# A fused gated MLP and per-sequence adapter kernel: reordered first steps and tail, and another order of ScalarE's two halves of each weight chunk

## The reference

```python
# layer 0: gated MLP with a conditioned norm; 127-level activations, ternary down weights
scale = cond @ norm_w.T + 1.0
ms = jnp.mean(x * x, axis=-1, keepdims=True)
h = x * (scale[:, None, :] * jax.lax.rsqrt(ms + EPS))
val, gate = jnp.split(h @ up_w.T, 2, axis=-1)
h = val * jax.nn.gelu(gate, approximate=False)
y = act_quant(h) @ weight_quant(down_w).T
x = y + x
# layer 1: adapter whose weights are generated from cond for each sequence
dWd = ((h_lang @ Wdd.T + bdd) * DELTA_SCALE).reshape(B, BN, D)
dWu = ((h_lang @ Wdu.T + bdu) * DELTA_SCALE).reshape(B, D, BN)
down = jax.nn.relu(jnp.einsum('bld,bnd->bln', x, Wd + dWd) + bd)
out = x + jnp.einsum('bln,bdn->bld', down, Wu + dWu) + bu
```

## Time and profile before

| | us |
|---|---|
| median of 3 runs | 473.05 (473.02 to 473.46) |
| profiled execution, its own time | 473.57 |
| its span, first to last instruction | 471.8 |
| busy in the span: PE | 464.3 (98%) |
| busy: DVE | 386.4 (82%) |
| busy: ACT | 364.3 (77%) |
| busy: POOL | 269.1 (57%) |

### The profile page before, as it was taken

The page is one execution under the profiler, slowest core; times in us unless marked ns, Lnnn a source line. Parts: engine busy times, 40 slices in busy tenths (PEclk is TensorE's granted clock), DMA queues, the critical chain, the costliest instruction groups (busy, mean ns, idle before and its releaser), DMA issues.

```text
span 471.8 us, 10035 instructions
## 1 busy us (share of the span) xinstructions
PE 464.3 (98%) x3276; PEld 269.3 (57%) x3276; DVE 386.4 (82%) x787; ACT 364.3 (77%) x636; POOL 269.1 (57%) x681
## 2 busy tenths in 40 slices
PE   8999999999999999999999999999999999999996
PEld 7445565665656555555555555555555555655564
DVE  3887798888989898788888887878888888777886
ACT  3788999999999967776777777686686787677664
POOL 1653558565675645465656546656555656544663
PEclk9999999999999999999999999999999999999999
DMA  7925588967778455535545445645535455444343
GB/s 259 392 80 111 135 206 200 260 182 217 182 236 243 104 103 120 106 100 162 130 133 157 91 124 136 166 122 136 137 84 162 124 145 147 113 105 119 101 81 110
DMA packets 118003, 70.99 MB, mean 150 GB/s; under 512 B 102016, under 2 KB 102976, under 8 KB 115904
## 3 DMA queue, kind: packets, MB, share of 16 engines
q1 hardware_dynamic: 117360, 69.63, 56.4%
q10 hardware_dynamic: 592, 0.73, 0.5%
HBM read 37.44 MB, written 8.39 MB: 97 GB/s over the span
## 4 chain that ended last, share of the span: by engine, by line
PE 91%; DVE 3%; DMA 1%; issue 1%; ACT 1%; POOL 1%; ACTq 0%; DVEq 0%; POOLq 0%
PE bank L1147 65%; PE bank L1161 11%; PE bank L1223 5%; PE bank L1255 4%; PE bank L1241 4%; DMA xT_s<-in_xT 1%; PE bank L1123 1%; PE bank L1129 1%; DVE up_lo L1020 0%; ACT gel L621 0%; DVE hid L857 0%; POOL nwt L463 0%; PE bank L1173 0%; DVE amax L865 0%; POOL rms L470 0%
## 5 line engine op out<-in xcount | busy, mean ns | idle before, releaser
L621 ACT ACTIVATE gel<-bank,rms 128x512 f32<-128x512 f32 x125 | 85.5, 685 | 87.3 <-PE bank L1147 84.4
L1147 PE MATMUL bank<-up_hi,xs_hi 128*128 128x512 f16 x492 | 146.3, 379 | 0.3 <-DVE hid L857 0.3
L1147 PE MATMUL bank<-up_lo,xs_hi 128*128 128x512 f16 x492 | 146.3, 379 | 0.0
L1147 PE MATMUL bank<-up_hi,xs_lo 128*128 128x512 f16 x492 | 146.3, 379 | 0.0
L857 DVE SCALAR_TENSOR_TENSOR hid<-bank,rms,gel 128x512 f32<-128x512 f32 x121 | 90.6, 749 | 62.3 <-ACT gel L621 61.5
L1147 PEld LDWEIGHTS bank<-up_lo,xs_hi 128*128 128x128 f16 x492 | 48.1, 98 | 58.1
L1147 PEld LDWEIGHTS bank<-up_hi,xs_lo 128*128 128x128 f16 x492 | 48.1, 98 | 58.0
L448 POOL TENSOR_TENSOR wsplit<-stage,wsplit 128x288 f16<-128x288 f32 x64 | 53.1, 859 | 42.1 <-ACT wsplit L593 42.1
L865 DVE TENSOR_REDUCE amax<-hid 128x1 f32<-128x1024 f32 x61 | 74.4, 1220 | 2.1
L634 ACT ACTIVATE hid<-hid,amax 128x1024 f32<-128x1024 f32 (+1 forms) x62 | 70.0, 1130 | 0.4 <-DVE amax L909 0.4
L1161 PE MATMUL bank<-tern,qT 128*128 128x256 bf16 x504 | 65.3, 273 | 0.8 <-DVE x L969 0.7
(11 more groups left out here) (145 smaller groups left out, 662.7 us busy)
## 6 DMA issues: line engine op xcount, KB each, us to landing
xn_s<-in_xn SPq DMA_DIRECT2D x32, 256.0 KB, 3.4
stage<-in_WddT SPq DMA_DIRECT2D x8, 1024.0 KB, 6.1
stage<-in_WduT SPq DMA_DIRECT2D x8, 1024.0 KB, 5.4
xT_s<-in_xT SPq DMA_DIRECT2D x31, 256.0 KB, 3.1
out<-out_s SPq DMA_DIRECT2D x30, 256.0 KB, 2.3
adapt<-in_up_wT SPq DMA_DIRECT2D x4, 512.0 KB, 7.8
x<-in_down_wT SPq DMA_DIRECT2D x2, 512.0 KB, 9.1
qT<-qn SPq DMA_TRANSPOSE x63, 2.7
```

The lines of the kernel that those rows point to most:

```text
L621: nc.scalar.activation(gel_of(t, c), u_banks(t, c)[1][:], ACT.Gelu, scale=rms[:, t // TPB % XN_SLOTS, t % TPB:t % TPB + 1]).then_inc(gelu_ ...
L1147: ins = nc.tensor.matmul(dst[:], a[:, t // TPB % 2, k, cols], w[:, c, k, v, :], start=(k == 0 and n == 0), stop=(k == KD - 1 and n == 2))
```

## The change

Three places are edited.

The first steps. SP issues the first x transfer (`xT_s[0]`) right behind the first of the four up weight pieces; before, ScalarE's queue issued it. The idle matmuls are 9 and 4 instead of 8 and 7. `up_first` is cut in two, and in the first column half the eight high passes of both tiles go ahead of the four low passes of either. The matmuls that sum the down weights' magnitudes stand after `up(2, 0)` instead of before `up(3, 0)`; ScalarE's `absolute_sum` and `squares(2)`, and VectorE's `ternary_first`, `rsqrt_guess(2)` and `ternary_second` move up accordingly. `base_sum` moves on GpSimd from the start to step 5, between the low parts of chunk 0 and chunk 1.

The chunks. ScalarE casts GpSimd's 1152 columns (behind the scaling that they need, on which it now has to wait) before it casts VectorE's 896.

The tail. Casting x to float16 for tiles 61 and 62 goes from ScalarE to VectorE, for tile 63 the other way. Tile 61 is turned in the middle of `down_last`; the turns of 62 and 63 move; sequence 31 goes in the order 0, 1. GpSimd makes the low part of tile 62 (VectorE did), and its output biases are spread out. ScalarE copies both turned halves of tile 63.

```diff
-IDLE_FIRST = 8
-IDLE_SECOND = 7
+IDLE_FIRST = 9
+IDLE_SECOND = 4
...
             for n in range(NC * KD):
                 sp.dma_start(raw_up[:, n // KD, n % KD], up_wT[:, n // KD, n % KD]).then_inc(ld_up[n], 16)
+                if n == 0:
+                    sp.dma_start(xT_s[:, 0], xT[0]).then_inc(ld_xT[0], 16)
...
             split_cond()
             rsqrt(1)
-            base_sum()
             rsqrt(2)
...
+                if s == FIRST + 1:
+                    base_sum()
...
             middle_low(B - 4)
             dequantization(LAST_T)
             residual_low(LAST_T - 2)
-            output_bias(B - 2)
+            output_bias_tile(B - 2, 1)
             middle_low(B - 3)
-
-            pool.wait_ge(x1_lo_done, LAST_T - 2)
+            residual_low(LAST_T - 1)
+            output_bias_tile(B - 2, 0)
+            output_bias_last(0)
             output_bias_last(1)
-            output_bias_last(0)
             middle_low(B - 2)
...
+                act.wait_ge(w_scaled, q + 1)
+                nc.scalar.copy(wsplit[:, q % 2, 0, first], stage[:, q % 2, first]).then_inc(w_hi_p, 1)
                 nc.scalar.activation(wsplit[:, q % 2, 0, rest], stage[:, q % 2, rest], ACT.Copy, scale=W_SCALE
                                      ).then_inc(w_hi_v, 1)
-                act.wait_ge(w_scaled, q + 1)
-                nc.scalar.copy(wsplit[:, q % 2, 0, first], stage[:, q % 2, first]).then_inc(w_hi_p, 1)
...
-            act.dma_start(xT_s[:, 0], xT[0]).then_inc(ld_xT[0], 16)
...
+            absolute_sum(0)
             gelu(0, 0)
             gelu(0, 1)
             gelu(1, 0)
+            absolute_sum(1)
             gelu(1, 1)
-            absolute_sum(0)
-            absolute_sum(1)
+            squares(2)
...
-            residual_high(LAST_T - 2)
+            relu(B - 3)
             qT_evacuate()
-            relu(B - 3)
-            residual_high(LAST_T - 1)
             x61_evacuate()
-            x63_hi_evacuate()
+            residual_high_last()
             relu(B - 2)
+            x63_evacuate()
             relu_last()
...
             gate(1, 1)
+            ternary_first()
             gate(2, 0)
+            rsqrt_guess(2)
             quant_scale(1)
             gate(2, 1)
-            ternary_first()
+            ternary_second()
             gate(3, 0)
-            rsqrt_guess(2)
             scaled_low(2)
...
             residual(LAST_T - 2)
-            total(B - 4)
+            residual_high(LAST_T - 2)
             qT_evacuate()
             residual(LAST_T - 1)
+            residual_high(LAST_T - 1)
             residual(LAST_T)
-            residual_high_last()
+            total(B - 4)
             residual_low(LAST_T)
-            residual_low(LAST_T - 1)
-            x63_lo_evacuate()
             x62_evacuate()
             total(B - 3)
...
                     pe.wait_ge(arrived, count)
+                    if n == 2:
+
+                        pe.wait_ge(late_lo_done, 3)
+                        x_transpose(LAST_T - 2, x61_ps, (0, 1))
...
                     up_first(0, s)
+                    if s == 1:
+                        up_first_end(0, s)
                     up_first(1, s)
+                    if s == 0:
+                        up_first_end(0, s)
+                    up_first_end(1, s)
                     continue
-                if s == 3:
+                up(s, 0)
+                if s == 2:
...
-            pe.wait_ge(late_lo_done, 3)
-            x_transpose(LAST_T - 2, x61_ps, (0, 1))
-
+            middle(B - 2)
+            pe.wait_ge(late_lo_done, 4)
+            x_transpose(LAST_T - 1, x62_ps, (0, 1))
             pe.wait_ge(last_x1_hi_done, 1)
             x_transpose(LAST_T, x63_hi_ps, (0,))
-            middle(B - 2)
+            output(B - 3)
             pe.wait_ge(x1_lo_done, LAST_T - 3)
             x_transpose(LAST_T, x63_lo_ps, (1,))
-            pe.wait_ge(x1_lo_done, LAST_T - 2)
-            x_transpose(LAST_T - 1, x62_ps, (0, 1))
-            output(B - 3)
+            middle_last(0)
             middle_last(1)
-            middle_last(0)
             output(B - 2)
             output_last()
```

More of the change, by code:

```diff
@@ L303, in build @@
         qT_v_done = sem("qT_v_done")
+        late_x1_hi_done = sem("late_x1_hi_done")
         last_x1_hi_done = sem("last_x1_hi_done")
@@ L494, in residual_low @@
             def residual_low(t):
-                pool.wait_ge(x1_hi_done, t + 1)
+                if t < LAST_T - 2:
+                    pool.wait_ge(x1_hi_done, t + 1)
+                else:
+                    pool.wait_ge(late_x1_hi_done, t - LAST_T + 3)
                 parts = x1n[:, t % X1N_SLOTS]
@@ L512, in output_bias, with output_bias_tile @@
                                             ).then_inc(outb_done, 1)
+            def output_bias_tile(b, i):
+                pool.wait_ge(x1_done, b * TPB + i + 1)
+                pool.wait_ge(stored[b % OUT_SLOTS], 16 * (b // OUT_SLOTS))
+                nc.gpsimd.tensor_tensor(out_s[:, b % OUT_SLOTS, i], x1[:, (b * TPB + i) % X1_SLOTS], bu_row[:], ALU.add
+                                        ).then_inc(outb_done, 1)
             def base_sum():
@@ L665, in x61_evacuate, with residual_high_last, x63_evacuate @@
                                ).then_inc(x61T_done, 1)
-            def x63_hi_evacuate():
+            def residual_high_last():
+                act.wait_ge(x1_done, LAST_T + 1)
+                act.wait_ge(x1T_done[LAST_T % X1N_SLOTS], slot_count(LAST_T - X1N_SLOTS, X1N_SLOTS))
+                nc.scalar.copy(x1n[:, LAST_T % X1N_SLOTS, 0], x1[:, LAST_T % X1_SLOTS]).then_inc(last_x1_hi_done, 1)
+            def x63_evacuate():
                 act.wait_ge(mid_full, LAST_B - X1T_SLOTS + 1)
-                act.wait_ge(x_turned, 2)
+                act.wait_ge(x_turned, 3)
                 nc.scalar.copy(x1T[:, LAST_B % X1T_SLOTS, 0:KD, 1],
                                x63_hi_ps[:, 0:KD * P].rearrange("p (c q) -> p c q", q=P)).then_inc(x63T_hi_done, 1)
+                act.wait_ge(x_turned, 4)
+                nc.scalar.copy(x1T[:, LAST_B % X1T_SLOTS, KD:2 * KD, 1],
+                               x63_lo_ps[:, 0:KD * P].rearrange("p (c q) -> p c q", q=P)).then_inc(x63T_lo_done, 1)
             def relu_last():
@@ L677, in relu_last @@
                 act.wait_ge(o_full, B - 2)
-                for n, i in enumerate(LAST_ORDER):
+                for i in range(TPB):
                     cols = slice(i * P, (i + 1) * P)
-                    act.wait_ge(mid_full, LAST_B + 1 + n)
+                    act.wait_ge(mid_full, LAST_B + 1 + i)
                     nc.scalar.activation(late_mid[:, cols], last_mid_ps[i][:, 0:P], ACT.Relu, bias=bd_col[:, 0:1],
@@ L740, in _ @@
                 if s == FIRST:
+                    squares(3)
                     gelu(s, 1)
-                    squares(3)
                 quantize(s - 1)
@@ L917, in quantize_last, with residual_high @@
                                         ).then_inc(last_qn_done, 1)
-            def residual_high_last():
-                dve.wait_ge(x1_done, LAST_T + 1)
-                dve.wait_ge(x1T_done[LAST_T % X1N_SLOTS], slot_count(LAST_T - X1N_SLOTS, X1N_SLOTS))
-                nc.vector.tensor_copy(x1n[:, LAST_T % X1N_SLOTS, 0], x1[:, LAST_T % X1_SLOTS]).then_inc(last_x1_hi_done, 1)
+            def residual_high(t):
+                dve.wait_ge(x1_done, t + 1)
+                dve.wait_ge(x1T_done[t % X1N_SLOTS], slot_count(t - X1N_SLOTS, X1N_SLOTS))
+                nc.vector.tensor_copy(x1n[:, t % X1N_SLOTS, 0], x1[:, t % X1_SLOTS]).then_inc(late_x1_hi_done, 1)
             def qT_evacuate():
@@ L947, in split_last @@
                 dve.wait_ge(o_full, B - 2)
-                for n, i in enumerate(LAST_ORDER):
+                for i in range(TPB):
                     cols = slice(i * P, (i + 1) * P)
-                    dve.wait_ge(relu_done, LAST_B * 2 + 1 + n)
+                    dve.wait_ge(relu_done, LAST_B * 2 + 1 + i)
                     nc.vector.tensor_copy(late_mid_hi[:, cols], late_mid[:, cols]).then_inc(last_mid_hi_done, 1)
-                    dve.wait_ge(last_mid_hi_done, n + 1)
+                    dve.wait_ge(last_mid_hi_done, i + 1)
                     nc.vector.tensor_tensor(late_mid_lo[:, cols], late_mid[:, cols], late_mid_hi[:, cols], ALU.subtract
@@ L956, in total_last @@
             def total_last():
-                for n, i in enumerate(LAST_ORDER):
-                    dve.wait_ge(o_full, LAST_B + 1 + n)
-                    dve.wait_ge(outb_done, LAST_B * TPB + n + 1)
+                for i in range(TPB):
+                    dve.wait_ge(o_full, LAST_B + 1 + i)
+                    dve.wait_ge(outb_done, LAST_B * TPB + i + 1)
                     nc.vector.scalar_tensor_tensor(out=late_out[:, i], in0=last_out_ps[i][:, 0:D], scalar=1.0 / A_SCALE,
@@ L1124, in up_first, with up_first_end @@
                                              start=(k == 0 and n == 0), stop=False)
```

(7 more changed lines are left out.)

18 lines of the change are left out of this document (4 added, 14 removed).

## The result

The changed kernel takes 470.73 us (median of 5 runs, 470.62 to 471.25) beside 473.05 us before (median of 5, 473.00 to 473.49): 2.32 us less, ratio 0.9950 (95% interval 0.9937 to 0.9963). The forecast was 471.0. The profiled execution took 470.62 us with a span of 468.9; that of before was 473.57 with 471.8, 2.95 more. These two executions differ by more than the medians, and the reason lies in the first ten microseconds.

The account below looks back on a forecast made before the run. The prediction took TensorE to bound the kernel (busy 464.3 of 471.8 us). Its terms, -0.3 - 1.0 - 0.6 - 0.15 = -2.05 us, took 473.05 to 471.0 us, range 470.1 to 472.2 with the clock and tail rivals.

Parts of the forecast that it names:

- Start, -0.3: Term for the start, up to tile 2: the new order of passes brings it 0.3 us earlier (-0.6 to +0.4).
- 44 passes follow from the second up piece: Start: 44 of the 48 passes of tiles 0 and 1 run from 10.60 at 0.216 us each, ending at 20.10.
- I take no shift: Start: the second up piece, though issued 0.65 us later, arrives when it did before; bounds -0.3 and +0.65.
- Steps 2 to 6, -1.0: Term for tile 2 to `down(3)`: gelu(4, 0)'s 0.88 us wait for GpSimd's root goes; 1.0 us gained (-1.3 to -0.4).
- Chunks, -0.6: Term for the chunk stage: exchanged casts remove `generate`'s waits of 0.73 us, less a new one; -0.6 (-0.73 to -0.1).
- The collision at chunk 1: Chunks: `base_sum` ahead of GpSimd's low part may make `generate` wait at chunk 1, 0.1 us, at most 0.5.
- Tail, -0.15: Term for the tail: TensorE's 1.06 us hole goes, GpSimd becomes what is waited for; -0.15 (-0.5 to +0.7).
- The clock did stay low: Rival, start, 13%: TensorE's clock rises 3 us later, +1.5 us, of which 0.3 is swallowed; 472.2 us.
- the rival for the tail and `base_sum`: Rival, 10%: GpSimd fills the tail and `base_sum` collides at chunk 1, +0.85 and +0.5 us on the forecast; 472.3 us.
- The early steps: Rival, steps 2 to 6, 5%: the ternary pass before gate(2, 0) makes VectorE late, the 1.0 us is lost; 472.0 us.
- VectorE falling behind: Rival, chunk stage, 4%: VectorE's low part is held beyond its spare 0.83 us per step; the kernel slows to 475.3 us.
- The chance for "faster": Whole kernel: 0.84 for faster, from the forecast, half the clock rival and half the others ending just under the line.

Follow-up runs that it names:

- b_notern: The kernel before with the new order of steps 2 to 6, but VectorE's three ternary passes in their old places: 472.13 us, ratio 0.9975.
- a_base: The changed kernel with `base_sum` moved forward into GpSimd's idle time behind the third amax product: 470.48 us, ratio 0.9937 against the kernel before.
- a_best: The changed kernel with both the edit of a_base and the edit of a_tail2: 470.59 us, ratio 0.9943 against the kernel before.
- a_cold: The changed kernel without any idle matmul (0 and 0 instead of 9 and 4): 473.70 us, ratio 1.0008 against the kernel before.
- b_steps: The kernel before with the new order of steps 2 to 6 alone, later `base_sum` included, casts in the old order: 472.19 us, ratio 0.9974.
- a_load: a_base with two added 128x256 casts on VectorE behind gate(s, 0) in each of 16 chunk steps: 475.32 us, ratio 1.0041 against the kernel before.
- a_again: The changed kernel as it is, measured once more: 470.93 us, ratio 0.9945 against the kernel before.
- a_tail2: The changed kernel with GpSimd's `middle_low(30)` ahead of its last bias operation: 470.84 us, ratio 0.9941 against the kernel before.
- a_xact: The changed kernel with the first x transfer back on ScalarE's queue: 471.46 us, ratio 0.9968 against the kernel before.

## Why the prediction was right, and where it was not

**Start, -0.3.** The step that 44 passes follow from the second up piece holds. In the new order tile 2 stands 9.67 behind the piece's first pass in every trace at the upper clock (10.78 or 10.79 behind the start of its cast); in the old order that cast is 11.05 to 11.09 ahead of tile 2. The step "I take no shift" for that piece was mis-sized: 0.48 earlier on the mean. The term is -0.8, outside its own bound of -0.6.

**Steps 2 to 6, -1.0.** Measured -1.14 from tile 2 to `down(3)`. That the wait for the root was the stall agrees with the traces of before and b_notern, though the guess was not moved alone. The ternary pass in the hole before gate(2, 0) gave nothing (b_notern), and the new wait before `up(3, 0)` is not there. The prediction counted some 1.7 us of holes and named only the last one; the gain came at three places (0.45, 0.28 and 0.43).

**Chunks, -0.6.** The exchange alone gives -0.81, the waits of 0.73 and a little more. The collision at chunk 1 was put at 0.1, at most 0.5; it is 0.51. Moved to the start that was measured, 1.05 earlier than forecast, the prediction has the low part end at 56.35 and TensorE want it at 56.95. TensorE did want it then, but the low part ended 0.83 later, at 57.18. Of that, 0.56 is chunk 1's four pieces, at 3.63 instead of 3.07 because the new order lays all of them beside VectorE's low part; `base_sum` took 4.4 instead of "some 4". Net -0.3.

**Tail, -0.15.** Measured -0.18 to -0.19, with the predicted wait for `middle_low(30)`. Here two misses cancel: VectorE's cast of tile 61 took 0.29 instead of 0.67, and GpSimd's eight operations were not back to back (0.23 of waiting for the cast of tile 62, and two bias operations in 1.60 instead of 1.41).

The sum of the sizes as measured is -0.8 - 1.14 - 0.3 - 0.18 = -2.4 against -2.05 forecast and -2.32 timed. The start's miss and the collision had opposite signs, so the total came out better than its terms; in that much the good forecast is luck.

**Rivals.** The clock did stay low for longer in two traces, at a price of 0.1 (a_base: 10.24 to 20.00) to 0.3 (a_best: 10.35 to 20.28), not 1.2; without idle matmuls at all it was 0.5 (a_cold). Of the rival for the tail and `base_sum` one half came true: the collision took its upper bound, the tail did not. The early steps gained what they should (b_steps). VectorE falling behind did not happen: its low part was 0.5 longer, 0.83 were to spare. The rule quoted from the Trainium skill (SBUF — State Buffer, section SBUF: two separate sides), by which VectorE is held for one piece at most, agrees: 0.5 against pieces of 0.7. a_load shows that the rival's price was real: with the budget used up the kernel is slower than before. The chance for "faster" is added up wrongly: 0.68, half of 0.13 and half of 0.15 are 0.82, not 0.84.

## What to carry to other kernels

Cut a trace at places where the bound engine runs without a break and compare distances between them: from tile 2 to the transposes of q, the five traces after, a_again, a_tail2, a_xact and a_cold agree to 0.01 us (438.32 or 438.33), while their whole times go from 470.52 to 472.83. When a change lays two engines' work side by side, price both with their durations beside each other, not with those of the old order. And measure the parts alone before crediting one: half of a reordering may be idle.
